# A transposed copy of x is loaded, and its mean rides as a ninth row in the logits' transfer

## What is computed

```python
# layer 0: graph attention, 8 heads of 64 units
h = relu(layernorm(x))
feats = einsum('bnf,hfu->bhnu', h, W);  e_self, e_neigh = feats.a_self, feats.a_neigh
dense = leaky_relu(e_self[..., :, None] + e_neigh[..., None, :], 0.2) + NEG_BIG * (1 - A)
x = x + relu(softmax(dense) @ feats + b)
# layer 1: two hypergraph convolutions, Din 512 -> Dh 1024 -> Dout 512
h = relu(layernorm(x))
r = relu(Dinv * H @ (Binv * H.T @ (h @ W1.T)) + b1)
y = Dinv * H @ (Binv * H.T @ (layernorm(r) @ W2.T)) + b2
out = x + (y + h)
```

## Time and profile before

| | |
|---|---|
| timed runs | 2608.23 us (2608.07 to 2610.93) |
| the profiled execution | 2608.28 us, its span on the core 2606.5 us |
| busy share of the span | PE 98%, weight loads 86%, DVE 72%, ACT 58%, POOL 56% |
| DMA engines | 11% of each slice after the first, 61 GB/s |
| mean granted clock of TensorE | 0.995 |

### The profile page before, as it was taken

How to read it: one execution, slowest core, us unless ns; L and a number is a source line. 1 busy time by engine, 2 the same in 40 slices (tenths; PEclk the granted TensorE clock), 3 DMA queues, 4 the chain that set the end, 5 groups by cost and what they waited for, 6 DMA issues and landing times.

```text
span 2606.5 us, 51365 instructions
## 1 busy us (share of the span) xinstructions
PE 2557.4 (98%) x15508; PEld 2245.3 (86%) x15508; DVE 1872.0 (72%) x4638; ACT 1503.2 (58%) x3593; POOL 1457.5 (56%) x2196
## 2 busy tenths in 40 slices
PE   4999999999999999999999999999999999999998
PEld 3788888888888888888888888888888888888886
DVE  6777777767777776777777777777777767777774
ACT  3565555556555555555655555565555555555553
POOL 5555555555555555555555555555555555555553
PEclk8999999999999999999999999999999999999999
DMA  4111111111111111111111111111111111111110
GB/s 152 52 56 66 61 55 63 59 61 61 60 61 55 63 59 61 63 59 61 55 65 58 58 63 59 61 57 64 61 55 63 59 61 62 59 61 55 63 54 25
DMA packets 85593, 158.70 MB, mean 61 GB/s; under 512 B 16832, under 2 KB 33216, under 8 KB 85568
## 3 DMA queue, kind: packets, MB, share of 16 engines
q1 hardware_dynamic: 85568, 158.39, 17.7%
HBM read 124.26 MB, written 34.08 MB: 61 GB/s over the span
## 4 chain that ended last, share of the span: by engine, by line
PE 96%; DVE 0%; issue 0%; POOL 0%; ACT 0%; POOLq 0%; DVEq 0%; ACTq 0%
PE p_w1a L800 14%; PE p_w1a L799 14%; PE p_w1a L804 13%; PE p_att L878 8%; PE p_w1b L800 5%; PE p_w1b L799 5%; PE p_w1b L804 5%; PE p_w1b L915 4%; PE p_att L858 4%; PE p_ta L825 4%; PE p_fa L793 2%; PE p_fa L794 2%; PE p_fa L795 2%; PE p_fb L794 2%; PE p_fb L795 2%; PE p_fb L793 2%
## 5 line engine op out<-in xcount | busy, mean ns | idle before, releaser
L359 POOL TENSOR_TENSOR rs<-ve,halfpow 128x1 f32<-128x1 f32 x128 | 115.3, 901 | 550.3 <-DVE ve L745 550.3
L799 PE MATMUL p_w1a<-W_hi,rT_hi 128*128 128x512 f32 x1024 | 416.4, 407 | 0.0
L800 PE MATMUL p_w1a<-W_lo,rT_hi 128*128 128x512 f32 x1024 | 406.0, 396 | 0.0
L424 ACT ACTIVATE att<-u,shifts 128x128 f32<-128x128 f32 x1024 | 399.7, 390 | 5.0 <-DVE shifts L705 5.0
L425 ACT ACTIVATE att_low<-u,shifts 128x128 f32<-128x128 f32 x1024 | 399.3, 390 | 0.0
L349 POOL TENSOR_TENSOR u<-u,mask 128x1024 f32<-128x1024 f32 x128 | 306.8, 2397 | 37.4 <-DMA u<-en_rows 27.2
L319 POOL TENSOR_TENSOR ve<-mv,eps 128x1 f32<-128x1 f32 x256 | 92.6, 362 | 401.2 <-DVE mv L630 321.9
L804 PE MATMUL p_w1a<-W_hi,rT_lo 128*128 128x512 f32 x1024 | 278.0, 393 | 0.0
L477 ACT ACTIVATE rT_hi<-p_tb 128x512 fp32r<-128x512 f32 x128 | 76.6, 598 | 331.2 <-PE p_tb L825 331.2
L760 DVE SCALAR_TENSOR_TENSOR z<-p_w1a,rs,t_bc 128x512 f32<-128x512 f32 x128 | 96.1, 751 | 218.9 <-PE p_w1a L804 218.9
L878 PE MATMUL p_att<-feats,attT 128*128 128x65 f32 x2048 | 243.2, 272 | 3.5 <-ACT attT L467 3.5
(11 more groups left out here) (127 smaller groups left out, 7235.6 us busy)
## 6 DMA issues: line engine op xcount, KB each, us to landing
u<-en_rows SPq DMA_DIRECT2D x128, 512.0 KB, 3.5
x_in<-in_x SPq DMA_DIRECT2D x128, 256.0 KB, 2.6
out<-raw SPq DMA_DIRECT2D x128, 256.0 KB, 2.1
adj_in<-in_adj SPq DMA_DIRECT2D x128, 128.0 KB, 2.4
en_rows<-eT SPq DMA_DIRECT2D x512, 1.0 KB
raw<-in_W1T SPq DMA_DIRECT2D x2, 1024.0 KB, 11.0
raw<-in_W2T SPq DMA_DIRECT2D x2, 1024.0 KB, 9.6
raw<-in_W0T SPq DMA_DIRECT2D x1, 1024.0 KB, 5.9
```

Of the source, the lines that this page charges most:

```text
L359: nc.gpsimd.tensor_tensor(rs1[:, :], ve1[:, :], halfpow[:, :], ALU.pow).then_inc(s_rs1, 1)
L424: nc.scalar.activation(att[:, i, :], u[:, g.slot(2), i, :], ACT.Exp, bias=shifts[:, 0, i:i + 1])
L799: mm(dst, hi, w_hi, start=first, stop=False)
L800: mm(dst, hi, w_lo, start=False, stop=False)
```

## The change

The host lays out a second copy of x, `xT`, in which each graph is transposed and cut in four blocks of 128 features. SP loads it (L240 of the changed kernel) into `xT_in`, 256 KB for each graph. The mean that must be subtracted then is needed along the free dimension and in every partition, as the logits are. So `bn_aggr` writes mean and variance into two columns of `e_blk`, `eT` gets a ninth row, `en_rows` and `u` become nine rows (`u` is 128 x 1152), and POOL subtracts `u`'s ninth row from `xT_in` into `xc`. ACT and DVE read `xc` in place of p_ta. The scale `rs0` is applied where DVE takes the features and logits out of PSUM. The statistics are made one turn earlier (graph t+5, at the end of DVE's turn), so the first turn is -5. PE's transposes of `xn`, ACT's `xn`, and POOL's `nm0` and `nb0` are gone. `rest`, `r` and `z` move into the buffer `raw`, which is free once the weights are split. The order of the first loads changes too.

The core of the diff:

```diff
@@ pool, turn @@
+                g = t.plus(3)
+                    pool.wait_ge(s_xT[g.slot(2)], g.uses(2, 16))
+                    pool.wait_ge(s_en_bc, g.count(per=16))
+                    nc.gpsimd.tensor_tensor(xc[:, :, :], xT_in[:, g.slot(2), :, :],
+                                            u[:, g.plus(2).slot(2), HEADS, :].unsqueeze(1).broadcast_to([P, DC, N]),
+                                            ALU.subtract).then_inc(s_xc, 1)
...
-                    pool.wait_ge(s_en_bc, g.count(per=16))
+                    pool.wait_ge(s_en_bc, g.plus(2).count(per=16))
@@ scalar, turn @@
+                    exps(t.plus(1), 1)
-                    act.wait_ge(s_xnT, g.count())
+                    act.wait_ge(s_xc, g.count())
-                    nc.scalar.activation(h0[:, :, 0, :], p_ta[:, :].rearrange("p (c n) -> p c n", n=N), ACT.Relu).then_inc(s_h0_hi, 1)
-                    exps(t.plus(1), 1)
+                    nc.scalar.activation(h0[:, :, 0, :], xc[:, :, :], ACT.Relu).then_inc(s_h0_hi, 1)
...
-                    nc.scalar.activation(xn[:, :], x_in[:, g.slot(4), :], ACT.Identity, bias=nb0[:, :],
-                                         scale=rs0[:, :]).then_inc(s_xn, 1)
@@ vector, turn @@
-                    nc.vector.tensor_copy(e_blk[:, 0:EW], p_fa[:, D2:D2 + EW]).then_inc(s_e_blk, 1)
+                    nc.vector.tensor_scalar(e_blk[:, 0:2 * SELF].rearrange("p (a n) -> p a n", a=2)[:, :, 0:HEADS],
+                                            p_fa[:, D2:D2 + EW].rearrange("p (a h) -> p a h", a=2), scale, None,
+                                            ALU.mult).then_inc(s_e_blk, 1)
...
+                g = t.plus(5)
+                    nc.vector.bn_stats(st0[:, :], x_in[:, g.slot(4), :]).then_inc(s_stats0, 1)
...
                     nc.vector.tensor_tensor(hg_lo[:, :], p_w1b[:, :], hg_hi[:, :], ALU.subtract).then_inc(s_hg_lo, 1)
+                if g.within(NG):
+                    nc.vector.bn_aggr(mv0, st0[:, :]).then_inc(s_mv0, 1)
@@ sync, turn @@
+                    load_xT(g)
...
-                        sp.dma_start(en_rows[:, 32 * q:32 * (q + 1)], eT[32 * q:32 * q + HEADS, :]).then_inc(s_en_out, 16)
+                        sp.dma_start(en_rows[:, 32 * q:32 * (q + 1)], eT[32 * q:32 * q + ROWS, :]).then_inc(s_en_out, 16)
...
-                                 en_rows.rearrange("(a h) n -> a (h n)", a=1).broadcast_to([P, HEADS * N])).then_inc(s_en_bc, 16)
+                                 en_rows.rearrange("(a h) n -> a (h n)", a=1).broadcast_to([P, ROWS * N])).then_inc(s_en_bc, 16)
@@ tensor, turn @@
                 if g.within(NG):
                     features(2, 0)
-                    features(2, 1)
...
                     last.then_inc(s_hg, 1)
                 g = t.plus(3)
                 if g.within(NG):
+                    features(2, 1)
                     features(3, 0)
                     features(3, 1).then_inc(s_feats, 1)
...
-                    pe.wait_ge(s_xn, g.count())
-                    transposes(p_ta, xn, s_xnT)
```

More of the change, by code:

```diff
@@ L115, in gnn_two_layers @@
         st2 = sb("st2", [P, 2, 6])
-        mv0 = sb("mv0", [P, 2])
         mv1 = sb("mv1", [P, 2])
@@ L162, in gnn_two_layers @@
         s_in = [sem(f"s_in{i}") for i in range(4)]
+        s_xT = [sem(f"s_xT{i}") for i in range(2)]
         s_out = [sem(f"s_out{i}") for i in range(2)]
@@ L352, in turn @@
                 if g.within(NG):
-                    rstd(g, mv2, ve2, rs2, s_mv2, s_ve2, s_rs2, s_z)
+                    if g.has(1):
+                        pool.wait_ge(s_z, g.count(1))
+                    rstd(g, mv2, ve2, rs2[:, :], s_mv2, s_ve2, s_rs2)
                 g = t.plus(1)
@@ L606, in turn @@
[L606 to L615 removed]
+                    feats_of(g, 0, scale)
@@ L616, in turn @@
+                if g.within(NG):
+                    feats_of(g, 1, scale)
                 g = t
@@ L838, in turn @@
                     pe.wait_ge(s_r, g.count(per=2) - 1)
-                    if g.plus(3).within(NG):
-                        pe.wait_ge(s_h0_lo, g.plus(3).count())
+                    if g.has(1):
+                        pe.wait_ge(s_rT_lo, g.count(1, per=2) - 1)
                     transposes(p_ta, r[:, 0:HALF], s_rT)
```

189 lines of the change are left out of this document (101 added, 88 removed).

## The result

The changed kernel takes 2590.12 us (median of 4 runs, 2588.91 to 2593.87), the kernel before beside it 2609.11 us (2608.07 to 2610.93): a ratio of 0.9931, 95% interval 0.9918 to 0.9943. It is 19 us faster where 37 were forecast. The time lies inside the range (2554 to 2596), but the likeliest case was wrong in size: half of the gain did not arrive. The profiled execution is the slowest of the four, 2593.87 us with a span of 2591.9.

A forecast was written before the change was run, and what follows sets the result against it. PE was taken to bound the kernel, busy 98% and without data waits in the middle turns. 2608.28 - 54.6 (transposes) + 3 (first turns) + 14 (stall) = 2570.7 us, forecast 2571, range 2554 to 2596.

The forecast's parts named there:

- the likeliest case: The forecast of 2571 us: stall in some turns, 2562 to 2585 us, chance 0.42.
- 124 x 0.44 = 54.6 us for the transposes: On PE: four transposes of xn take 0.44 us a turn, gained in 124 turns, 54.6 us.
- hg_hi keeps its cover at no cost: ACT's hg_hi before hidden: its cover on PE shrinks by 0.08 us, 0.42 us are left, no cost.
- The room at L915 decides: PE's L915 waits for ACT's h: 0.64 us of room, 0.28 left after coming 0.36 earlier; this path decides.
- Rival 2: A stall in every turn because the broadcast scales in full or more: 40 us and up, 2585 to 2603, chance 0.18.
- `eT` stands 0.15 us later behind `bn_aggr` and the scaled form: On DVE: bn_aggr, between 0.10 and 0.17 us, and a scaled instead of plain addition delay eT by 0.15 us.
- The trip: From eT's start to POOL's addition: limit 6.24 us; 6.48 in 59 turns waiting for the DMA, 61 wait only for POOL's mask.
- Stall in 59 turns, none in the others: At L915: 59 turns exceed the limit by 0.24 us, 14 us; the others, within 0.09 of it, cost nothing.
- its 19.35: PE's turn in the chain where L915 doesn't wait: 19.35 us, against 19.79 before.
- Other engines at nothing: Changed work on POOL, ACT, DVE and the DMA loads costs nothing while the idle times named hold.
- The hazard: DVE's h0 low, both inputs in SBUF, meets POOL's mask: up to 0.4 us could go; costed at nothing.
- First turns +3: In the first turns, xc behind W_lo delays features and later work: 3 us, between 0 and 10.

The follow-up runs named there:

- c_both_links: The changed kernel with hg_lo behind eT on VectorE and features(2, 1) ahead of the product of h and G again: 2578.94 us, ratio 0.9886.
- k_eight_rows: The changed kernel without the mean's row travelling to HBM and back, the centring subtracting a row of ones instead: 2580.64 us, ratio 0.9893.
- e5_before_one_transpose: The kernel before with three of the four transposes of xn left out from turn 0 on: 2571.96 us, ratio 0.9857.
- g3_all: The changed kernel with hg_lo behind eT, features(2, 1) ahead of the product, the late wait last, and first-turn weights loaded later: 2571.49 us, ratio 0.9857.
- g2_wait_order: The changed kernel with hg_lo behind eT and VectorE's wait for the last features behind those for eT, shifts and rs0: 2581.56 us, ratio 0.9898.
- g4_first_turns_two: The changed kernel with graph 1's eT earlier and W1's second half and all of W2 loaded behind graph 2's rows: 2586.57 us, ratio 0.9917.
- f7_first_turns: The changed kernel with graph 1's eT amid VectorE's set-up of W_a and 3 MB of weights loaded behind its rows: 2601.30 us, ratio 0.9975.

## Why the prediction was wrong

Point by point, by its own steps:

- **124 x 0.44 = 54.6 us for the transposes.** Slightly too much. Three of four gave 0.30 us a turn, 0.10 each, so about 0.40 for four, an estimate: 49 us.
- **hg_hi keeps its cover at no cost.** Right: no wait for it in the middle turns of the changed kernel. The move of features(2, 1) was hardly needed, though: with it undone in c_both_links TensorE's turn is 19.48.
- **The room at L915 decides.** Right as the place, and so is the chain behind it. Rival 2's form came true (a stall in every turn), but not by its reason, the broadcast.
- **The failed step: `eT` stands 0.15 us later behind `bn_aggr` and the scaled form.** This was all that the prediction allowed for the way from the product to `eT` (its 0.08 moves `eT` against the hidden layer and is no part of this way; the sentence has it the wrong way round, since `hidden` comes 0.08 sooner after the product, but the subtraction is right). Measured: 3.299 - 2.853 = 0.446 us, three times as much. Of this 0.28 lie between `hg_lo` and `eT` (1.13 before, 1.41 after), of them 0.09 `bn_aggr` and 0.1 the scaled instructions; in the first turn of each pass of the loop this part is 0.27 longer than in the others (0.08 before), which no run explains. Another 0.10 lie between the starts of `hg_hi` and `hg_lo` (0.63 before, 0.73 after): there `hg_lo` now stands behind four waits and not one, which no run takes apart. The last 0.07 lie ahead of `hg_hi`: the product itself gets longer when `h` is only just in time. And the way is double: over the features behind the product, which the moved features(2, 1) had made longer, `eT` would have come only 0.06 to 0.09 sooner. A way that was long enough to bind was priced by its two added instructions and not by the queue that they stand in.
- **The trip: 6.48 us in 59 turns, at most 6.33 in the others.** Too long. It takes 2.490 + 3.668 = 6.16 us in the mean, as before (6.17). The reading of the 59 and the 61 turns was right: 6.25 and 6.10 us in the trace of before. The broadcast grew by about 0.1 and not 0.22: 3.51 to 3.60 us from issue to landing in the mean, and k_eight_rows shows no gain worth the name without the row. That growth fell into a cushion: in the 61 turns the rows had landed at 3.36 us and the addition began at 3.62, behind the mask; now it begins 0.07 after each landing.
- **Stall in 59 turns, none in the others.** Wrong. The ring sets the pace of all middle turns. The prediction itself had the 61 others 0.09 us over the limit and took nothing for them. With means in place of the two kinds of turn its own ring is 2.853 + 0.15 + 6.17 + 0.22 + 10.14 = 19.53 us, 0.18 above its 19.35 and not 0.11 (14 us over 124 turns). From there to the measured 19.59 the misses at `eT` (+0.30) and in the trip (-0.23) nearly cancel. That the time still fell inside the range is owed to this, and is luck.
- **Other engines at nothing.** Right, for the reason given. The hazard was real: `h0` low takes 0.89 us with both inputs in SBUF (0.68 before), a mask on POOL beside it 0.79 (0.40); it costs the turn nothing: the column from the mask to the end of `h` is 10.035 against 10.033 in e5_before_one_transpose. What was not free are the statistics of x ahead of `hg_lo`, if the 0.10 us named above are their waits. The DMA engines had been 17% busy in the middle turns of before, and not the 11% of the table or a tenth; the larger load still left room.
- **First turns +3.** Wrong: 10.8 us, just beyond the upper bound, and by the mechanism that stood at that bound: small transfers behind the loads of the weights.

The balance by spans: 26.1 us less between turn 1 and turn 127 (forecast 54.6 - 14 = 41 less), 10.8 more in the first turns (3), 0.7 more at the end; -14.6, from 2606.5 to 2591.9. Of the 15 us missing in the middle turns 6 to 11 are TensorE's own pace (19.40 to 19.44 for 19.35), the rest the stall (0.15 to 0.19 us above that pace, for 0.11). Whether the last 0.04 us of this, between e5's 19.40 and g3_all's 19.44, belong to the changed order on TensorE was not tried.

## What to carry to other kernels

When an edit frees the engine that binds, draw the closed ring through the other engines, sum it with its handovers, and price every instruction and every wait that the edit puts on it; where a step hangs on two links that end together, undo both in one run, since each alone shows little. In a queue, put the wait that ends last behind those that are long fulfilled. And compare variants of a kernel that hangs on a DMA's latency only beside the kernel itself, in one group of runs on one chip.

## What the runs showed of the hardware

- The same kernel took 2583, 2590 and 2602 us in three groups of runs, while one broadcast of 576 KB landed in 3.5, 3.6 and 3.7 us; the kernel before, bound by TensorE, was the same within 0.05%. How much the change brings depends on it: 0.3 to 1.0%. Whether chip or occasion sets the landing is open.
- Three fulfilled waits behind a late one cost VectorE's queue 0.15 us (g2_wait_order), some 0.05 each.
- A group of products whose weights come just in time takes 0.97 to 1.02 us for 0.89, in most turns without a wait of PE (14 such waits in 122 turns); the weight loads' waits (12.4 us in all) show part of it.
- Four writes of about 1 KB each are followed by the broadcast that waits for their landing after 0.9 us on a quiet queue (middle turns, and g4_first_turns_two in a first turn), and after 2.4 to 6.8 us behind megabytes of x and weights on the same queue (6.8 at the second trip of f7_first_turns, 18.18 + 1.61 to 26.57).
